# The column network of a decoder layer, per sequence for all columns, against once at the end over tokens sorted by pair of columns

## The reference

```
logits = l2norm(x) . l2norm(col_emb) + sigmoid(gelu(x @ gate_w1 + gate_b1) @ gate_w2 + gate_b2)
k = max(1, int(16 * 0.05))                        # 1: one column per token
mask = one_hot(top_k(logits, k))
weights = mask * softmax(logits)
cols = gelu(einsum('bsd,cdn->bscn', x, W_cols) + b_cols)      # 16 columns of 64 neurons
y = (cols * weights).reshape(..., 1024) @ proj_w + proj_b + x
out = layernorm(y) * ln_g + ln_b ;  result = layernorm(x + out)
```

## Time and profile before

| | before |
|---|---|
| median of 3 runs | 2329.41 us (2327.68 to 2330.34) |
| the profiled execution | 2329.89 us, of which the span of its instructions is 2327.9 us |
| PE busy | 2219.2 us, 95% |
| DVE / ACT / POOL busy | 1678.1 / 1404.4 / 768.9 us |
| granted TensorE clock, mean | 0.984 |
| chain that ended last | PE 55%, DVE 22%, ACT 18%, issue 4%, POOL 1% |

### The profile page before, as it was taken

The page is one execution under the profiler, slowest core; times in us unless marked ns, Lnnn a source line. Parts: engine busy times, 40 slices in busy tenths (PEclk is TensorE's granted clock), DMA queues, the critical chain, the costliest instruction groups (busy, mean ns, idle before and its releaser), DMA issues.

```text
span 2327.9 us, 82936 instructions
## 1 busy us (share of the span) xinstructions
PE 2219.2 (95%) x33994; PEld 1901.7 (82%) x34026; DVE 1678.1 (72%) x5322; ACT 1404.4 (60%) x4326; POOL 768.9 (33%) x1771
## 2 busy tenths in 40 slices
PE   5899999999999999999999999999999999999986
PEld 4788888888888888888888888888888888888875
DVE  4577777777777777777777777777777777777753
ACT  3576555776555776555776555776555776555742
POOL 2332324333324332324332324333323333324321
PEclk8899999999999999999999999999999999999997
DMA  6000000000000000000000000000000000000000
GB/s 221 7 2 10 9 10 9 9 2 10 10 9 9 9 2 9 10 9 9 9 2 9 10 10 9 9 2 10 9 10 9 9 2 9 10 9 9 7 4 3
DMA packets 25065, 30.75 MB, mean 13 GB/s; under 512 B 8529, under 2 KB 21857, under 8 KB 23921
## 3 DMA queue, kind: packets, MB, share of 16 engines
q1 hardware_dynamic: 24688, 25.46, 3.3%
HBM read 21.25 MB, written 4.19 MB: 11 GB/s over the span
## 4 chain that ended last, share of the span: by engine, by line
PE 55%; DVE 22%; ACT 18%; issue 4%; POOL 1%; DVEq 0%; POOLq 0%
PE bank_b L644 10%; PE bank_a L460 6%; PE bank_b L736 5%; PE bank_b L652 5%; DVE acc L1010 4%; PE bank_a L542 4%; DVE diag L1046 3%; PE bank_b L673 3%; DVE y1p L1140 3%; DVE u L1087 3%; PE bank_a L581 3%; PE bank_a L572 3%; ACT prob L923 2%; ACT acc L814 2%; PE bank_a L532 2%
## 5 line engine op out<-in xcount | busy, mean ns | idle before, releaser
L1010 DVE SCALAR_TENSOR_TENSOR acc<-ypad,convw,acc 128x128 f32<-128x128 f32 x1536 | 432.2, 349 | 73.0 <-ACT acc L814 72.7
L460 PEld LDWEIGHTS bank_a<-xnT,wqkvz 128*128 128x128 f32 x2048 | 242.6, 195 | 43.3 <-DVE u L1087 42.8
L460 PE MATMUL bank_a<-xnT,wqkvz 128*128 128x128 f32 x2048 | 258.9, 281 | 17.1 <-DVE u L1087 17.1
L911 ACT ACTIVATE y1T<-bank_b 128x256 f32<-128x256 f32 x32 | 12.3, 384 | 313.0 <-PE bank_b L666 313.0
L1417 POOL TENSOR_SCALAR lnv<-mv 128x1 f32<-128x1 f32 x128 | 31.1, 243 | 509.5 <-DVE mv L1101 506.9
L923 ACT ACTIVATE prob<-bank_b,nmax 128x128 f32<-128x128 f32 x512 | 179.7, 374 | 2.2 <-DVE nmax L1160 1.8
L814 ACT ACTIVATE acc<-bank_a,convw 128x128 f32<-128x128 f32 x512 | 149.4, 405 | 0.0
L1321 POOL TENSOR_TENSOR gate<-ba,dtb 128x8 f32<-128x8 f32 x32 | 6.5, 203 | 430.3 <-ACT ba L825 430.3
L1158 DVE TENSOR_REDUCE smax<-bank_b 128x4 f32<-128x512 f32 x128 | 87.8, 686 | 68.5 <-PE bank_b L683 68.5
L736 PEld LDWEIGHTS bank_b<-y2T,wc 128*128 128x128 f32 x1024 | 124.3, 195 | 14.4 <-issue 14.4
L903 ACT ACTIVATE prob<-bank_b 128x512 f32<-128x512 f32 x64 | 38.2, 597 | 160.1 <-PE bank_b L644 160.1
(11 more groups left out here) (244 smaller groups left out, 5845.3 us busy)
## 6 DMA issues: line engine op xcount, KB each, us to landing
xin<-in_x_dram SPq DMA_DIRECT2D x32, 128.0 KB, 2.1
cin<-in_ctx_dram SPq DMA_DIRECT2D x32, 128.0 KB, 2.1
out_dram<-yout SPq DMA_DIRECT2D x32, 128.0 KB, 2.9
wqkvz<-in_wqkvz_dram SPq DMA_DIRECT2D x6, 512.0 KB, 6.8
wout<-in_wout_dram SPq DMA_DIRECT2D x1, 1024.0 KB, 9.8
wg<-in_wg_dram SPq DMA_DIRECT2D x1, 1024.0 KB, 11.4
wu<-in_wu_dram SPq DMA_DIRECT2D x1, 1024.0 KB, 13.4
wd<-in_wd_dram SPq DMA_DIRECT2D x1, 1024.0 KB, 15.2
```

The lines of the kernel that those rows point to most:

```text
L460: last = mm(A[bank][:, b * P:(b + 1) * P], wqkvz[:, c, o:o + P], xnT[:, c, :], start=(c == 0), stop=(c == KC - 1))
L1010: stt(acc[:, c, :], ypad[:, c, k:k + P], convw[:, c, k:k + 1], acc[:, c, :], ALU.mult, ALU.add).then_inc(conv.sem, 1)
```

## The change

Inside the trips the column network is gone. `c_pair` and `c_rank` and `c_pos` come in its place: the pair of columns of each token, its rank among all tokens so far with the same pair (a product with a triangle of ones, and a product of ones with the counts `seen`), and from it a row number. GpSimd scatters a row of 771 floats for each token (y2, y2 + proj_b, y2 + ln_b, its number, its weight, its side of the pair) to a region of `rows_dram` for its pair (`c_scat`). Behind the last trip each engine has an `ending`. VectorE computes from the counts which 128 rows each of 39 blocks takes and which pair it belongs to (`e_plan`, 20 instructions in a chain); GpSimd writes 8 times 128 padding rows behind the regions' ends; SP loads the 39 blocks, with the row number read into a register, into 11 slots; TensorE computes for each block the 128 neurons of its one pair, with the weights addressed by a register, and its projection; GpSimd scatters 39 times 128 rows of the result to the output by token number. 39 is (32 x 128 + 8 x 127) / 128, enough for any counts. `ORDER` is another one too. The bias comes in as a product of ones with a diagonal matrix.

```diff
-    pe="a_la10@1 a_la11@1 b_router@2 b_gu0@2 b_gu1@2 a_lb10@1 b_gu2@2 b_gu3@2 a_lb11@1 a_la20@1 b_dn0@2 "
...
-       "c_wT a_ss c_spread a_st a_kk a_dec1 c_pj0 b_oT0 c_pj1 b_oT1 b_w0 b_w1 a_la00 a_la01 b_cT a_qk b_v "
...
+       "c_pT3 a_o0@1 a_qkv1 a_o1@1 c_R c_pv a_z0 c_xo a_z1 a_qkv2 a_ss c_y2T a_qkv3 c_h a_st c_lg a_qk "
+       "a_dec0 a_dec1 c_rank a_kk b_oT0 b_oT1 b_w0 b_w1 b_cT a_la00 a_la01 a_lb00 a_lb01 b_v b_x2T a_la10 "
...
-                    pe.wait_ge(*gcw_ok(n - 1))
+                    pe.wait_ge(*pos(n - 1))
...
+            def load_block(b):
+                if b >= SLOTS:
+                    sp.wait_ge(y3_ok.sem, 4 * (b - SLOTS) + 2)
+                row = sp.value_load(blk_i[0:1, 0, b:b + 1], min_val=0, max_val=PAIRS_C * REGION)
+                sp.dma_start(slots[b % SLOTS], rows_d[bass.DynSlice(row, P), :]).then_inc(slot_in[b % SLOTS][0], 16)
...
+            sp.wait_ge(scattered.sem, 16 * (B + PAIRS_C))
+            sp.wait_ge(planned.sem, PLANNED)
+            for b in range(BLOCKS):
+                load_block(b)
+            sp.wait_ge(outs.sem, 16 * BLOCKS)
...
-            def columns(n, half):
...
-            def c_wT(n):
...
-            def c_spread(n):
...
-            def mix(n, half):
...
+            def c_rank(n):
+                if first(n):
+                    pe.wait_ge(wout_ok.sem, 2)
+                else:
+                    pe.wait_ge(*pos(n - 1))
+                pe.wait_ge(*pair_ok(n, 1))
+                mm(Bk[0][:, 0:PAIRS_C], con("upto"), pairs1[:, :], start=True, stop=False)
+                mm(Bk[0][:, 0:PAIRS_C], ones[:, :], seen[:, :], start=False, stop=True).then_inc(rank_ps.sem, 1)
+
+            def e_T(b):
+                pe.wait_ge(*slot_full(b))
+                if b >= 4:
+                    pe.wait_ge(*e_gT_ok(b - 3))
+                for c in range(KC):
+                    last = tr(A[b % 4][:, c * P:(c + 1) * P], slots[b % SLOTS][:, c * P:(c + 1) * P], ident)
+                last.then_inc(y2T_ps.sem, 1)
+
+            def e_columns(b, pair):
+                pe.wait_ge(side_ok.sem, b + 1)
+                if b >= 4:
+                    pe.wait_ge(*e_st(3 * (b - 4) + 1))
+                mm(Bk[b % 4][:, 0:P], ones[:, :], e_diag[b % 4], start=True, stop=False)
+                pe.wait_ge(*e_xT_ok(b + 1))
+                for c in range(KC):
+                    last = mm(Bk[b % 4][:, 0:P], e_xT[b % 4][:, c, :], wc[:, c, bass.DynSlice(pair * P, P)],
+                              start=False, stop=(c == KC - 1))
+                last.then_inc(c_ps.sem, 1)
+
+            def e_turn(b):
+                pe.wait_ge(gcw_ok.sem, b + 1)
+                tr(A[b % 4][:, 2 * P:3 * P], e_gw[b % 4], ident).then_inc(hg_ps.sem, 1)
+
+            def e_mix(b, pair):
+                pe.wait_ge(*e_gT_ok(b + 1))
+                mm(Bk[b % 4][:, D:2 * D], e_gT[b % 4], wp_flat[:, bass.DynSlice(pair * D, D)], start=True, stop=True)\
+                    .then_inc(pj_ps.sem, 1)
+
+            def ending():
+                pe.wait_ge(*pos(B))
+                mm(Bk[0][:, 0:PAIRS_C], ones[:, :], seen[:, :], start=True, stop=True).then_inc(rank_ps.sem, 1)
+                pe.wait_ge(planned.sem, PLANNED)
+                pairs = {}
+                for s in range(BLOCKS + 3):
+                    if s < BLOCKS:
+                        e_T(s)
+                    if 0 <= s - 3 < BLOCKS:
+                        e_mix(s - 3, pairs[s - 3])
+                    if 0 <= s - 1 < BLOCKS:
+                        pairs[s - 1] = pe.value_load(blk_i[0:1, 1, s - 1:s], min_val=0, max_val=PAIRS_C - 1)
+                        e_columns(s - 1, pairs[s - 1])
+                    if 0 <= s - 2 < BLOCKS:
+                        e_turn(s - 2)
...
+            def e_xTc(b):
+                act.wait_ge(*e_T_ps(b + 1))
+                fn(e_xT[b % 4], A[b % 4][:, 0:D].rearrange("p (c q) -> p c q", q=P), ACT.Copy).then_inc(y2T_ok.sem, 1)
+
+            def e_gelu(b):
+                act.wait_ge(c_ps.sem, b + 1)
+                if b >= 4:
+                    act.wait_ge(gcw_ok.sem, b - 3)
+                fn(e_g[b % 4], Bk[b % 4][:, 0:P], ACT.Gelu).then_inc(gc_ok.sem, 1)
+
+            def e_gTc(b):
+                act.wait_ge(*e_gT_ps(b + 1))
+                fn(e_gT[b % 4], A[b % 4][:, 2 * P:3 * P], ACT.Copy).then_inc(hT_ok.sem, 1)
+
+            def e_norm1(b):
+                act.wait_ge(*e_rs1(4 * (b // GROUP) + 4))
+                fn(e_y4[b % RING], e_y3[b % RING], ACT.Identity, scale=e_r[:, 0, RST, b:b + 1], bias=e_r[:, 0, NMR, b:b + 1])\
+                    .then_inc(c_yn.sem, 1)
+
...
+            def ending():
+                act.wait_ge(planned.sem, PLANNED)
+                for s in range(BLOCKS + LATE2):
+                    if s < BLOCKS:
+                        e_xTc(s)
+                    if 0 <= s - 1 < BLOCKS:
+                        e_gelu(s - 1)
+                    if 0 <= s - 2 < BLOCKS:
+                        e_gTc(s - 2)
+                    if 0 <= s - LATE2 < BLOCKS:
+                        e_norm2(s - LATE2)
+                    if 0 <= s - LATE1 < BLOCKS:
+                        e_norm1(s - LATE1)
...
-                nc.vector.reciprocal(lsm[:, 3:4], lsm[:, 2:3]).then_inc(lchain.sem, 1)
-
-            def gated(n, half):
...
+            def c_pair(n):
+                dve.wait_ge(*lchain(n, 5))
+                both = onehot[:, :].rearrange("p (j v) -> p j v", v=2)
+                tt(pairs1[:, :], both[:, :, 0], both[:, :, 1], ALU.add).then_inc(pair_ok.sem, 1)
+                nc.vector.tensor_reduce(yrow[:, SIDE:SIDE + 1], both[:, :, 1], AX_X, ALU.add).then_inc(pair_ok.sem, 1)
+
+            def c_pos(n):
+                dve.wait_ge(*rank_ps(n))
+                nc.vector.tensor_tensor_reduce(out=rankw[:, :], in0=pairs1[:, :], in1=Bk[0][:, 0:PAIRS_C], scale=1.0,
+                                               scalar=0.0, op0=ALU.mult, op1=ALU.add, accum_out=rowf[:, :])\
+                    .then_inc(pos.sem, 1)
+                tt(seen[:, :], seen[:, :], pairs1[:, :], ALU.add).then_inc(pos.sem, 1)
+                dve.wait_ge(*pos(n, 1))
+                nc.vector.tensor_copy(rowi[:, :], rowf[:, :]).then_inc(pos.sem, 1)
...
+            def e_sides(b):
+                dve.wait_ge(*slot_full(b))
+                nc.vector.tensor_copy(tok_i[:, b:b + 1], slots[b % SLOTS][:, ID:ID + 1])
+                if b >= 4:
+                    dve.wait_ge(c_ps.sem, b - 3)
+                ts(e_diag[b % 4], ident, e_bias[:, b:b + 1], None, ALU.mult).then_inc(side_ok.sem, 1)
+
+            def e_gate(b):
+                dve.wait_ge(gc_ok.sem, b + 1)
+                if b >= 4:
+                    dve.wait_ge(*e_gT_ps(b - 3))
+                stt(e_gw[b % 4], pln("side"), slots[b % SLOTS][:, SIDE:SIDE + 1], e_g[b % 4], ALU.is_equal, ALU.mult)\
+                    .then_inc(gcw_ok.sem, 1)
+
+            def e_sum(b):
+                dve.wait_ge(pj_ps.sem, b + 1)
+                if b >= RING:
+                    dve.wait_ge(*e_n1(b - RING + 1))
+                slot, y = slots[b % SLOTS], e_y3[b % RING]
+                stt(y, Bk[b % 4][:, D:2 * D], slot[:, WEIGHT:WEIGHT + 1], slot[:, D:2 * D], ALU.mult, ALU.add).then_inc(c_bn.sem, 1)
+                dve.wait_ge(*e_st(3 * b + 1))
+                nc.vector.bn_stats(e_bn[:, b, :], y).then_inc(c_bn.sem, 1)
+                dve.wait_ge(*e_st(3 * b + 2)).then_inc(dve_passed.sem, 1)
+                nc.vector.bn_aggr(e_mv[:, 0, b, :], e_bn[:, b, :]).then_inc(c_bn.sem, 1)
+
+            def e_affine(b):
+                dve.wait_ge(*e_n1(b + 1))
+                slot, y = slots[b % SLOTS], e_y4[b % RING]
+                tt(y, y, rows[:, LG, :], ALU.mult).then_inc(y3_ok.sem, 1)
+                dve.wait_ge(y3_ok.sem, 4 * b + 1)
+                tt(y, y, slot[:, 2 * D:3 * D], ALU.add).then_inc(y3_ok.sem, 1)
+                dve.wait_ge(y3_ok.sem, 4 * b + 2)
+                nc.vector.bn_stats(e_bn[:, b, :], y).then_inc(y3_ok.sem, 1)
+                dve.wait_ge(y3_ok.sem, 4 * b + 3).then_inc(dve_passed.sem, 1)
+                nc.vector.bn_aggr(e_mv[:, 1, b, :], e_bn[:, b, :]).then_inc(y3_ok.sem, 1)
+
+            def ending():
+                e_plan()
+                for s in range(BLOCKS + LATE1 + 1):
+                    if s < BLOCKS:
+                        e_sides(s)
+                    if 0 <= s - 1 < BLOCKS:
+                        e_gate(s - 1)
+                    if 0 <= s - 3 < BLOCKS:
+                        e_sum(s - 3)
+                    if 0 <= s - LATE1 - 1 < BLOCKS:
+                        e_affine(s - LATE1 - 1)
...
+            def c_scat(n):
+                pool.wait_ge(*y2b_ok(n))
+                pool.wait_ge(*lchain(n))
+                pool.wait_ge(*pair_ok(n))
+                pool.wait_ge(*pos(n))
+                nc.gpsimd.indirect_dma_start(rows_d[:, :], bass.IndirectOffsetOnAxis(rowi[:, 0:1], 0), yrow[:, :], None)\
+                    .then_inc(scattered.sem, 16)
...
```

(29 more changed lines are left out.)

297 lines of the change are left out of this document (186 added, 111 removed), and 6 rows, old and new, of tables (dve, pe).

## The result

The changed kernel takes 2391.18 us (median of 4 runs, 2386.68 to 2396.18) against 2328.76 us for the kernel before in the same comparison: 1.0268 times as long, with a 95% interval of 1.0246 to 1.029. I had forecast 2309 us and a gain. The time lies 82 us above the forecast and 25 us above the upper end of the range. The profiled execution took 2396.18 us, of which 2394.4 are span.

A forecast was written before the change was run, and what follows sets the result against it. TensorE's queue was taken to set the 69.7 us trip. First slot 2332.1, plus blocks 140.4, plus edges 9.6, minus 175 (31 trips at 5.65), gives 2307, plus 2.0 outside the span: 2309 us; range 2260 to 2366, 8 in 10.

The forecast's parts named there:

- What leaves and comes into the trips: PE work per trip: 8.1 us of columns, mask and projection leave, 0.45 of c_rank comes; net 7.65 us.
- New gaps of 2.0 us: PE idle added per trip, from the gate-to-solve chain, a_ss and the experts' part; ends 0 and 3.5 us.
- c_scat costs the trips nothing: One GpSimd scatter issue per trip is free, as that engine has 45 us free; cost 0.
- The start of the ending: From the last sequence's mark through plan, scatter and paddings to the first load: first slot full at 2332.1 us.
- X: Time of one GpSimd scatter or padding issue, in no trace row: 1.2 us, ends 0.24 and 2.9.
- One block: One of the ending's 39 blocks: VectorE slowest at 3.5 us, taken as 3.6; 140.4 us for all.
- T: Time per block step in the ending, set by VectorE: 3.6 us, for 3.5 and a few waits.
- In front of and behind the blocks: Ending's edges: 3.5 us before the first sum, 6.1 us for the last block's norm, issue and landing.
- PE stays packed: Rival for the trips: only 0.5 us of gaps added, time 2262 us; chance 0.14.
- The chain eats the trip: Rival at the gate-to-solve chain: new gaps 3.5 us, time 2355; decides from 2.7 us of gaps; chance 0.16.
- TensorE sets the ending: Rival for the ending: low clock makes a block near 4.4 us, time 2340; decides from 4.15; chance 0.18.
- GpSimd sets the ending: Rival for the ending: issues of 2.4 us, 4.15 per block, time 2341, or 2365 at 2.9; chance 0.10.

The follow-up runs named there:

- e6_plain: Changed kernel with the trips' scatter replaced by one plain SyncE store to consecutive rows, sorting left out; 2391.23 us, 1.0271 times the kernel before.
- e3_old_order: Changed kernel with all four engines' order lines of the kernel before, new steps put in, new ending kept; 2521.84 us, 1.0834 times the kernel before.
- e5_pause: Changed kernel with one VectorE wait, after the second group of taps, for GpSimd's first output-scale instruction; 2334.24 us, 1.0023 times the kernel before.

## Why the prediction was wrong, by its own steps

**What leaves and comes into the trips: right in kind, a little high.** I had net 7.65 us of PE work; the busy time of an undisturbed trip fell by 6.6 (68.21 in a plain trip before, 61.65 after). The removed instructions stood 7.9 us wide; c_rank stands 0.44 wide, as estimated (0.45). Less busy time went than width, for part of the removed instructions' printed time overlapped their neighbours': 7.2 us of a trip's busy time were theirs alone. So net 7.65 was 1.1 us too high, measured by busy time.

**New gaps of 2.0 us: the step that failed.** In an undisturbed trip PE is idle 4.04 us instead of 1.3, so new gaps are 2.7, and 1.6 of them stand before a_qkv2, where I had looked for no gap, since "VectorE, ScalarE and GpSimd lose work as well, but they are busy 75%, 62% and 34% of a trip, so I count nothing for it". An engine busy 34% or 75% of a trip can still hold another one up in one place: GpSimd's product lay 3.35 us longer under VectorE's run. The places that I had named hold less. From c_lg to a_la00 (1027.90 to 1037.98) it is 10.08 us, near the chain's 10.25, but TensorE's work there fills all of it but 0.25, where I had 9.5. In front of a_ss PE waits 0.15 a trip. The experts' part has the 0.5 I gave it (L712, 0.46). The largest other gap, 0.8 us more than before inside the solve (L628), has no cause in the profile.

**The clock: no term.** The gap before a_qkv2 also brought the granted clock down in 11 of 29 trips, another 0.78 us per trip. The prediction had asked what a lower clock does in the ending only.

**Per trip: gain 5.65 predicted, 3.38 measured (69.85 - 66.47).** With the pause it is 69.85 - 64.54 = 5.31, near the forecast, and that is in part luck: 1.1 us too much removed work stand against new gaps that are then 1.2 instead of 2.0. The last c_pos came at 2211.0 instead of near 2137; 62.5 us of these 74 the pause takes away (the last c_sum2 at 2138.4 instead of 2200.9), 4.8 of them ahead of the first c_sum2.

**c_scat costs the trips nothing: right** (e6_plain), though the reason that I gave, 45 us free on GpSimd, would have let a second one pass too, and that one costs 45 to 72 us.

**The start of the ending: right.** X was 1.2, measured 0.96 to 1.12 plus 0.30; from c_pos to the first slot 20 predicted, 19.8 measured, with nine issues in 11.4 instead of 10.8.

**One block: right.** T was 3.6, measured 3.52 in the middle; VectorE's own 3.5 is 3.23. The first and last three steps are shorter, so the blocks take less than the 140.4 of the sum: 128.1 us from the first to the last sum.

**In front of and behind the blocks: too short.** From the first slot to the end of the span I had 150.0 us (3.5 + 140.4 + 6.1), and it is 163.5. From the first slot to the first sum it is 8.9, in a stretch where the granted clock is 0.67. Behind the last sum I had 6.1 us. The stretch from the end of its statistics:

```profile
2369.10:2394.40 25.30, 0.00 (x0) 0.00 (x0) 5.68 (x17) 4.96 (x9) 14.11 (x28) 0.50 0.06 18
```

25.3 us, since GpSimd was two groups behind: it goes on with five norms and seven stores, 4.3 to 6.1 us from one pair of stores to the next, the last issue at 2386.65, 7.7 us before the end. I had priced its queue as a rate (2.95 of 3.6) and not asked where it stands when VectorE is through.

**The account.** 2391 - 2309 = 82: 57 for the hold-up and the clock that it costs, 13.5 for the ending behind its first slot, and 31 x (5.65 - 5.31) = 10.5 for the trip's other terms, 81 in all.

**The rivals.** PE stays packed: no. The chain eats the trip: its bound of 2.7 us of new gaps was reached, but the chain that ate the gain goes from GpSimd over a_core to a_qkv2; the one that I described appears in the old order alone (e3_old_order). TensorE sets the ending: no, T stays under 4.15 with the clock at 0.87 from the first to the last sum. GpSimd sets the ending: not by a long issue, but the order of its queue costs the steps 0.29 us each and stretches the end. I had weighed the Trainium skill's "DVE blocks DMA" box (page "SBUF — State Buffer") for it; here an issue takes 0.96 to 1.10 us beside the packed VectorE of the ending, up to 1.26 in the trips, and 0.96 beside an idle one. So no issue was held up by more than 0.3 us; whether VectorE ran in a two-port mode beside one, no row tells. The sentence of the same page of the Trainium skill quoted further up was the one that bore on this case.

## What to carry to other kernels

When a reordering puts VectorE instructions with two inputs from SBUF back to back, look for small GpSimd instructions whose operand gets ready inside the run, read in the trace how long they take there (some pass, one here did not), and see who waits for them: the busy share of either engine says nothing on it. A wait in the middle of the run, for a value that is needed soon anyway, can be worth far more than it costs. Where the last work of a kernel is in groups, count how many groups each engine is behind when the bound engine ends, since that is the length of the tail.

## What the hardware did that I had not expected

- A GpSimd product of 128 x 4 values took 3.26 to 3.58 us instead of 0.20, in 29 of 32 trips, and ended 0.06 us after VectorE's run of 20 scalar_tensor_tensor; with a pause in the run its median is 0.40 and its maximum 0.70. A product of the same shape later in that run (L1604 of e5_pause) takes 0.38, and the power between them its 1.03 us, as elsewhere.
- With a gap of 2.1 us on PE in each trip of 66 the granted clock was 0.97 in nine of 29 trips and 0.93 in two, for about 14 us in the trips; with 8 unread products in the gap it was 1.00 in 28 of 29.
- With a second indirect DMA issue per trip on GpSimd, PE stops for 0.45 to 0.47 us inside a step of 32 x 32 products beside an issue, 13 to 24 us more in all, and the kernel takes 45 to 72 us longer; with a plain second write of the same bytes it doesn't. The cause is open.
